# First product of the experts as three products of rounded high and low parts

## What is computed

```python
def _L0_ffn_ref(x, w_g, c_fc, c_proj):          # 8 experts, top 2, 640 places each
    ...
    exp_batches = jnp.einsum('tec,td->ecd', sec_mask, xt)          # rows sorted to the experts
    h = jax.nn.gelu(jnp.einsum('ecd,edf->ecf', exp_batches, c_fc), approximate=False)
    exp_out = jnp.einsum('ecf,efd->ecd', h, c_proj)
    out = cb_weight.reshape(T, N_EXP * cap) @ exp_out.reshape(N_EXP * cap, d)
    ...
```

## Time and profile before

| | us |
|---|---|
| median of 3 runs | 496.49 |
| lowest and highest | 496.16, 497.43 |
| span of the profiled execution | 505.8 |

### The profile page before, as it was taken

How to read it: one execution, slowest core, us unless ns; L and a number is a source line. 1 busy time by engine, 2 the same in 40 slices (tenths; PEclk the granted TensorE clock), 3 DMA queues, 4 the chain that set the end, 5 groups by cost and what they waited for, 6 DMA issues and landing times.

```text
span 505.8 us, 7932 instructions
## 1 busy us (share of the span) xinstructions
PE 434.7 (86%) x2766; PEld 302.8 (60%) x2766; DVE 299.7 (59%) x712; ACT 228.6 (45%) x351; POOL 257.2 (51%) x321
## 2 busy tenths in 40 slices
PE   7887695868778899999989999888966989999980
PEld 6534252425677778888965333335545967888860
DVE  4899899998520313215696999899954201211354
ACT  4867673433110352242167998876842013224220
POOL 5897785898648854565340000022546533455470
PEclk9999996978979999999999999999987899999996
DMA  5455473991342211225613434594011121221266
GB/s 136 141 196 209 143 256 98 330 280 38 75 163 68 74 60 55 78 58 192 189 42 95 99 95 101 143 277 154 28 37 43 38 79 42 63 76 55 73 228 209
DMA packets 50327, 60.87 MB, mean 120 GB/s; under 512 B 7152, under 2 KB 29296, under 8 KB 50288
## 3 DMA queue, kind: packets, MB, share of 16 engines
q1 hardware_dynamic: 42672, 47.50, 31.8%
q0 software_dynamic: 4608, 8.47, 5.2%
q10 hardware_dynamic: 3008, 4.40, 2.7%
HBM read 29.78 MB, written 25.31 MB: 109 GB/s over the span
## 4 chain that ended last, share of the span: by engine, by line
PE 30%; issue 20%; SPq 15%; DMA 6%; DVE 4%; POOL 1%; another core or an unknown queue 1%; ACT 1%; POOLq 0%; ACTq 0%; DVEq 0%
PE ps L1354 26%; SPq L390 12%; SPq L322 3%; PE ps L1510 2%; DMA chosen_y<-ye,y_to 2%; DMA last_got<-chosen_y 1%; DMA got<-chosen_y 1%; PE ps L1358 1%; POOL chosen_y L552 1%; DMA xe<-slots_x 1%; DVE xn L1249 1%; DMA slots_x<-rows_x,put_at 0%; DVE stats L1238 0%; DVE xres L1178 0%
## 5 line engine op out<-in xcount | busy, mean ns | idle before, releaser
L552 POOL DMA_INDIRECT chosen_y<-ye,y_to x80 | 78.8, 985 | 77.0 <-DVE ye L1224 56.1
L729 ACT ACTIVATE hT<-ps 128x640 f32<-128x640 f32 x64 | 45.1, 704 | 86.2 <-issue 53.3
L502 POOL DMA_INDIRECT slots_x<-rows_x,put_at x64 | 62.9, 982 | 41.3 <-issue 19.4
L1358 PE MATMUL ps<-ident 128*128 128x128 f32 x576 | 75.7, 293 | 5.6 <-POOL head_of L423 2.1
L1278 DVE SCALAR_TENSOR_TENSOR feat<-expo,ps 128x1024 f32<-128x1024 f32 x64 | 76.4, 1217 | 3.7 <-ACT expo L858 3.3
L858 ACT ACTIVATE expo<-ps,minus_one 128x1024 f32<-128x1024 f32 x64 | 70.4, 1116 | 12.9 <-PE ps L1354 9.0
L1358 PEld LDWEIGHTS ps<-ident 128*128 128x128 f32 x576 | 70.5, 152 | 8.5 <-issue 3.7
L1354 PE MATMUL ps<-cproj_sb,hT 128*128 128x128 f32 x640 | 74.6, 275 | 0.3
L1354 PEld LDWEIGHTS ps<-cproj_sb,hT 128*128 128x128 f32 x640 | 73.0, 192 | 0.9 <-issue 0.6
L1354 PE MATMUL ps<-xeT,cfc_sb 128*128 128x320 f32 x256 | 71.7, 433 | 2.1 <-DVE xeT L1189 2.1
L1189 DVE COPY xeT<-ps 128x640 f32<-128x640 f32 x16 | 13.2, 825 | 93.6 <-PE ps L1510 46.3
(11 more groups left out here) (230 smaller groups left out, 603.7 us busy)
## 6 DMA issues: line engine op xcount, KB each, us to landing
chosen_y<-empty_rows SPq DMA_DIRECT2D x32, 256.0 KB
decay<-k_rows SPq DMA_DIRECT2D x30, 256.0 KB, 5.4
stk<-part SPq DMA_DIRECT2D x96, 64.0 KB, 2.0
slots_x<-empty_rows SPq DMA_DIRECT2D x16, 325.0 KB, 6.3
xe<-slots_x SPq DMA_DIRECT2D x16, 325.0 KB
cfc_sb<-in_L_ffn_c_fc SPq DMA_DIRECT2D x2, 2048.0 KB
got<-chosen_y SPq DMA_DIRECT2D x8, 256.0 KB
got<-chosen_y ACTq DMA_DIRECT2D x8, 256.0 KB
```

The lines of the kernel that those rows point to most:

```text
L502: pool.indirect_dma_start(out=slots_x[k], out_offset=bass.IndirectOffsetOnAxis(ap=put_at[:, c, kk, t:t + 1], axis=0), in_=rows_x[:, kk * N ...
L552: pool.indirect_dma_start(out=chosen_y[k], out_offset=bass.IndirectOffsetOnAxis(ap=y_to[:, b, i:i + 1], axis=0), in_=ye[:, b, i * D:(i + 1 ...
L729: act.activation(hT[:, b, f, :].rearrange("p (a n) -> p a n", a=2), ps[:, 2 + 2 * (f % 2):4 + 2 * (f % 2), 0:HALF], ACT.Gelu).then_inc(h_r ...
L1358: pe.transpose(ps[:, bank, 0:P], ident[:], ident[:])
```

## The change

The first product takes its operands in the type float32r, which PE multiplies in one record instead of two. To keep the precision, weights and rows are each split into a rounded high part and the rest: high weights by high rows, low weights by high rows, and high weights by low rows are added up in PSUM. ACT rounds (`weights_high`, `rows_high`), DVE subtracts (`weights_low`, `rows_low`), one expert ahead. The split weights of two experts and the low rows lie in the space of `stk`, so its ones are set after the layer's first products. `rows_high` takes the place of the copy to `xeT`; `stack_proj` moves behind expert 2's gelus.

```diff
-            stk = sb("stk", [STK, NB, NG, BK], F32R, mb)
+            room = sb("room", [P, NB * NG * BK], F32R, mb)
+            stk = room[0:STK, :].rearrange("p (c g t) -> p c g t", c=NB, g=NG)
+            cfc_hi = room[:, 0:2 * FF].rearrange("p (b f) -> p b f", b=2)
+            cfc_lo = room[:, 2 * FF:4 * FF].rearrange("p (b f) -> p b f", b=2)
+            xe_lo = room[:, 4 * FF:4 * FF + 2 * CAP].rearrange("p (b n) -> p b n", b=2)
...
-            xeT = sb("xeT", [P, 2, CAP], F32, m)
+            xe_hi = sb("xe_hi", [P, 2, CAP], F32R, m)
...
+        weights_split = lambda s: 2 * s + 1
+        rows_split = lambda s: 2 * s + 2
...
# POOL
-                    pool.memset(stk[3 * GR:STK, :, :, :].bitcast(F32), 1.0).then_inc(stk_ones, 1)
-                    pool.wait_ge(stk_ones, 2)
...
             experts(0)
+            pool.wait_ge(h_mm, NE * NF)
+            pool.memset(stk[3 * GR:STK, :, :, :].bitcast(F32), 1.0).then_inc(stk_ones, 1)
+            pool.wait_ge(stk_ones, 2)
...
# ACT
+                def weights_high(e):
+                    s = k * NE + e
+                    if e == 0:
+                        act.wait_ge(cfc_in, 16 * (k + 1))
+                    if s >= 2:
+                        act.wait_ge(h_mm, (s - 1) * NF)
+                    copy(cfc_hi[:, e % 2, :], cfc_sb[:, e, :]).then_inc(high_ready, 1)
+
+                def rows_high(e):
+                    s = k * NE + e
+                    act.wait_ge(xe_turned, s + 1)
+                    if s >= 2:
+                        act.wait_ge(h_mm, (s - 1) * NF)
+                    copy(xe_hi[:, e % 2, :], flat(ps[:, 0:2, :])[:, 0:CAP]).then_inc(high_ready, 1)
+
+                weights_high(0)
+                rows_high(0)
                 for e in range(NE):
...
                     act.activation(slot_w[:, b, :], xe[:, b, :, D + 1], ACT.Tanh, scale=0.5).then_inc(share_ready, 1)
-                    if s == 2:
-                        stack_proj()
+                    if e + 1 < NE:
+                        weights_high(e + 1)
                     for f in range(NF):
...
                                        ACT.Gelu).then_inc(h_ready, 1)
+                    if e + 1 < NE:
+                        rows_high(e + 1)
+                    if s == 2:
+                        stack_proj()
...
# DVE
-                def turned_in(e):
+                def weights_low(e):
...
+                    dve.wait_ge(high_ready, weights_split(s))
...
-                    dve.tensor_copy(xeT[:, b, :], flat(ps[:, 0:2, :])[:, 0:CAP]).then_inc(xeT_ready, 1)
-
-                turned_in(0)
+                    dve.tensor_tensor(cfc_lo[:, b, :], cfc_sb[:, e, :], cfc_hi[:, b, :].bitcast(F32),
+                                      ALU.subtract).then_inc(low_ready, 1)
+
+                def rows_low(e):
...
+                    dve.wait_ge(high_ready, rows_split(s))
...
+                    dve.tensor_tensor(xe_lo[:, b, :], flat(ps[:, 0:2, :])[:, 0:CAP], xe_hi[:, b, :].bitcast(F32),
+                                      ALU.subtract).then_inc(low_ready, 1)
+
+                weights_low(0)
+                rows_low(0)
                 for e in range(NE):
...
                     if e + 1 < NE:
-                        turned_in(e + 1)
+                        weights_low(e + 1)
...
                     dve.wait_ge(y_to_ready, s + 1)
+                    if e + 1 < NE:
+                        rows_low(e + 1)
...
# PE
-                        pe.wait_ge(xeT_ready, s)
+                        pe.wait_ge(low_ready, rows_split(s - 1))
...
-                pe.wait_ge(cfc_in, 16 * (k + 1))
...
-                    pe.wait_ge(xeT_ready, s + 1)
+                    pe.wait_ge(high_ready, rows_split(s))
                     for f in range(NF):
                         if s * NF + f >= 2:
                             pe.wait_ge(h_ready, s * NF + f - 1)
-                        for a_ in range(2):
-                            ins = mm(ps[:, 2 + 2 * (f % 2) + a_, 0:HALF], cfc_sb[:, e, f * P:(f + 1) * P],
-                                     xeT[:, b, a_ * HALF:(a_ + 1) * HALF])
+                        for n, (w, rows) in enumerate(((cfc_hi, xe_hi), (cfc_lo, xe_hi), (cfc_hi, xe_lo))):
+                            if f == 0 and n == 1:
+                                pe.wait_ge(low_ready, weights_split(s))
+                            if f == 0 and n == 2:
+                                pe.wait_ge(low_ready, rows_split(s))
+                            for a_ in range(2):
+                                ins = mm(ps[:, 2 + 2 * (f % 2) + a_, 0:HALF], w[:, b, f * P:(f + 1) * P],
+                                         rows[:, b, a_ * HALF:(a_ + 1) * HALF], start=n == 0, stop=n == 2)
```

More of the change, by code:

```diff
@@ L207, in program @@
             ("ln_stat", "ln_mv", "ln_std", "ln_rstd", "ln_shift", "ln_out", "xn_turned", "xnT_ready")))
-        wT_mm, wT_ready, wbeta_ready, wv_ready = sem("wT_mm"), sem("wT_ready"), sem("wbeta_ready"), sem("wv_ready")
+        wT_mm, wT_ready, spread_ready = sem("wT_mm"), sem("wT_ready"), sem("spread_ready")
         qk_mm, beta_mm, gate_mm, sq_ready, raw_ready, sumsq_mm = (
@@ L228, in program @@
         ye_out = [sem(f"ye_out{i}") for i in range(2)]
-        xe_turned, xeT_ready, h_mm, h_ready, ye_mm, ye_ready = (
-            sem(n) for n in ("xe_turned", "xeT_ready", "h_mm", "h_ready", "ye_mm", "ye_ready"))
+        xe_turned, high_ready, low_ready, h_mm, h_ready, ye_mm, ye_ready = (
+            sem(n) for n in ("xe_turned", "high_ready", "low_ready", "h_mm", "h_ready", "ye_mm", "ye_ready"))
         rows_made, ids_made, y_to_ready, share_ready = (
@@ L751, in _ @@
             copy(wbeta[:].rearrange("p (h d) -> p h d", d=HD),
-                 wall[:, 3 * D:QKVB].unsqueeze(2).broadcast_to((P, H, HD))).then_inc(wbeta_ready, 1)
+                 wall[:, 3 * D:QKVB].unsqueeze(2).broadcast_to((P, H, HD))).then_inc(spread_ready, 1)
             turned_x(0, 5)
@@ L755, in _ @@
                  wall[:, 2 * D:3 * D].rearrange("p (h i) -> p i h", i=HD).unsqueeze(3).broadcast_to((P, HD, H, HD))
-                 ).then_inc(wv_ready, 1)
+                 ).then_inc(spread_ready, 1)
             square_half(0, 1)
@@ L1181, in experts @@
             def experts(k):
-                def turned_in(e):
+                def weights_low(e):
                     b = e % 2
                     s = k * NE + e
-                    dve.wait_ge(xe_turned, s + 1)
+                    dve.wait_ge(high_ready, weights_split(s))
                     if s >= 2:
                         dve.wait_ge(h_mm, (s - 1) * NF)
-                    dve.tensor_copy(xeT[:, b, :], flat(ps[:, 0:2, :])[:, 0:CAP]).then_inc(xeT_ready, 1)
-                turned_in(0)
+                    dve.tensor_tensor(cfc_lo[:, b, :], cfc_sb[:, e, :], cfc_hi[:, b, :].bitcast(F32),
+                                      ALU.subtract).then_inc(low_ready, 1)
+                def rows_low(e):
+                    b = e % 2
+                    s = k * NE + e
+                    dve.wait_ge(high_ready, rows_split(s))
+                    if s >= 2:
+                        dve.wait_ge(h_mm, (s - 1) * NF)
+                    dve.tensor_tensor(xe_lo[:, b, :], flat(ps[:, 0:2, :])[:, 0:CAP], xe_hi[:, b, :].bitcast(F32),
+                                      ALU.subtract).then_inc(low_ready, 1)
+                weights_low(0)
+                rows_low(0)
                 for e in range(NE):
@@ L1550, in _ @@
             pe.wait_ge(wall_in, 16 * 4)
-            pe.wait_ge(wbeta_ready, 1)
+            pe.wait_ge(spread_ready, 1)
             pe.wait_ge(xnT_ready[0], 1)
@@ L1556, in _ @@
             project_q(0)
-            pe.wait_ge(wv_ready, 1)
+            pe.wait_ge(spread_ready, 2)
             repeat_v(0)
```

## The result

The changed kernel takes 491.77 us (median of 14 runs, 489.33 to 497.2) beside 496.05 us for the kernel before in the same session: a ratio of 0.9935, 95% interval 0.9913 to 0.9957, so 3.2 us less (2.1 to 4.3). The medians themselves lie 4.3 us apart; this text goes by the ratio, which comes with an interval and leaves out the one slow run, at 497.2. The forecast was 491.8. In a second session the same kernel came out at 492.90 beside 494.16, a ratio of 0.9978 (0.9951 to 1.0006), so 1.1 us less (-0.3 to 2.4). So the time is right. The gain is smaller than the 4.7 us forecast, which lies outside both intervals; the two sessions don't agree well on it, and the second alone would not show one. What follows shows why: two of the forecast's steps went another way, in opposite directions.

A forecast was written before the change was run, and what follows sets the result against it. PE was taken to bound the expert layers; 0.58 us gained per later expert, less 1.36 in each first one and a cut at layer 2's end, made 4.7 us: 496.49 to 491.8 us, range 488.3 to 495.2.

The forecast's parts named there:

- The product: First product on PE: each float32r product of 320 columns takes 0.148 us (0.144 to 0.151), six making 0.89 a block.
- rival without extra: First product on PE: 0.133 us a product, by columns alone, so 488.3 us; chance 0.10.
- slower rival: First product on PE: weight loads not overlapped, 0.255 us a product, about 527 us in all; chance 0.06.
- The stop ahead of the third block: First product, each expert: PE stands 0.17 us because the first block's gelu must empty the bank pair.
- Copies, subtractions and memset at nothing: ACT's and DVE's added work mid-layer and POOL's moved memset cost nothing; cover some 2 us, for the memset 1.2.
- The first expert: First expert of each layer: two exposed table loads on ACT make it 1.36 us later (1.30 to 1.39).
- rival of a hidden tail: Table loads on ACT: 1.2 to 1.6 us unrecorded on each of four, 496.5 to 498.3 us; chance 0.03.
- The clock: Rival, first expert: PE's clock falls in its idle time, 1.7 us a layer, 493.5 or 495.2 us; chance 0.23.
- Layer 2's end: Last two experts of layer 2: early adds on DVE hold `ye`, so only 0.5 of 1.16 us gained counts.
- The sum: Both layers: 2.7 us gained in layer 1 and 2.0 in layer 2, together 4.7 us (4.0 to 5.7).
- The loads are not exposed: Rival, first expert: table loads shared or early, it loses only some 0.3 us, so 489.7 us; chance 0.06.

The follow-up runs named there:

- two terms: Changed kernel without the product of high weights by low rows, 16 records in place of 24, all copies and subtractions kept; 483.5 us, ratio 0.978.
- old product: Changed kernel with all copies, subtractions, waits and moved memset, but the first product in float32 as before, one per half; 497.45 us, ratio 1.0058.
- gelu column: Changed kernel plus one gelu of a 128x1 column on ACT ahead of weights_high(0) in both layers; 486.15 us, and 486.33 in another session.
- gap filled: Changed kernel plus 15 dummy transposes on PE between the second and third block of each layer's first expert; 488.64 us, ratio 0.9884.

## Why the prediction came out as it did

**The product: right.** 0.148 us was forecast (0.144 to 0.151), 0.148 measured, so 0.015 of extra on 320 columns beside 0.017 on 512. The rival without extra falls. All weight loads lie under the products, so the slower rival falls too.

**The stop ahead of the third block: right.** 0.17 forecast, 0.17 in the profile, and with two terms 0.47, both from 1.06 between the first block's end and the third's start. Period 8.75 forecast, 8.73 measured.

**Copies, subtractions and memset at nothing: right.** Periods of 9.32 with all of them and the old product. The cover measured 2.84 us where I said some 2. The memset and the normalisation behind it, by POOL's and DVE's timelines, stand against the earlier trace rows:

```profile
238.10 6.93 POOL L587 MEMSET room<- 1x8192 f32 x1
...
246.29 1.34 DVE L1290 TENSOR_SCALAR xn<-xres,mv,rstd 128x128 f32<-128x128 f32 x4
```

It ends at 245.03, 1.26 us ahead of an unchanged normalisation.

**The first expert: right at full clock.** 1.36 us later was forecast; 1.34 and 1.24 were measured (7.50 at full clock in either layer, against 6.16 and 6.26). The chain has ACT's steps in the order and lengths of the forecast. Behind the load the Tanh follows after 0.01 us, so the rival of a hidden tail falls. With it falls the Trainium skill's drain of about 1380 ns (ScalarE: Activation LUTs, "What ACT_TABLE_LOAD costs"), which no load here shows whose next instruction was ready. The same page of the Trainium skill, in its section "Table sets: the hidden batching unit", lists the Tanh with the sets of exp and sigmoid and not with gelu's; here the Tanh ran behind the gelu's load without one of its own, and the gelu column used that.

**The clock: the step that failed.** I gave a fall in the first expert 0.23 and priced one at 1.7 us. The price was right (1.6 measured). The chance was not: with the stop of 1.76 us it fell in three of four first experts, with 2.6 and 3.6 us in four of four. With the stop filled or removed it fell in one of twelve, with the stop of 1.6 (old product) in none of two, in the kernel before in none of four. "Products stand close on both sides" was no argument against it. That the stop raises the chance of a fall is shown, on these few first experts, by taking it away in two ways; that it is the only cause is refuted by the one fall without it, whose cause stays open. With falls in three of four layers the forecast's gain drops by 2.4 us. By these counts the likeliest case was a fall in at least one layer, in the prediction's own prices 493.5 or 495.2.

**Layer 2's end: the step that failed the other way.** Only 0.5 of 1.16 us was to count, because the early adds end at 486.73 and `ye` starts at 487.25. The mechanism exists: in the second profile of the changed kernel `ye` comes 10.85 us after the last transposes, so the last expert gains nothing there. But the row was one draw. Over the profiles of the kernel before, the changed one, the gap filled and the gelu column, the second add of layer 2 starts 8.0 to 10.3 us after the last transposes, late where its rows land late; in layer 1 of the same profiles it starts at 8.0 to 8.1 each time. In the first profile of the changed kernel, with the gap filled and in one of the two of the gelu column all 0.58 us of the last expert counted (10.20 to 10.24 in place of 10.81). The forecast treated a fetch's landing as fixed.

**The sum.** Without falls the layers give 72.89 - 70.09 = 2.80 and 73.00 - 70.12 = 2.88, 5.7 us, where 4.7 was forecast, and the kernel with the gap filled measured 5.7. The difference of 1.0 is layer 2's end (0.66) and first experts and periods a little better than forecast (0.3). Falls take 1.6 each off it: three in four layers leave 3.3, and the ratio says 3.2 in the first session and 1.1 in the second. That the median met the forecast to 0.1 us is luck: one error of 1.0 and one of 2.4 in opposite directions stand behind it. What lies behind each layer varies too: from layer 1's last `ye` to the normalisation were 11.96 and 10.82 us in the two profiles of the kernel before and 11.72 to 12.56 in those of the changed one, the gap filled and the gelu column, so the agreement of 5.7 with 5.7 is good to its interval and no further.

**A rival priced wrongly.** "The loads are not exposed" was put at 489.7, on a first expert that still loses 0.3. With the gelu column it gains 0.5 to 0.6, as the other experts do. PE waits 0.89 us for the copy to `xe_hi` where it waited 1.01 for the one to `xeT`, and the wait for the low rows costs some 0.2. The two loads were worth 1.9 us a layer, and 1.6 more where the clock fell. "Every load in the trace speaks against" was misread: the kernel before has two loads at the Tanh's line for its 16 Tanhs, so all but the first of each layer ran behind gelus without one. That one set serves both could be seen in it.

## What to carry to other kernels

A step put ahead of an activation with its own table moves the load behind the step's wait. Ask in what order the engine meets its first use of each table, and let a column of the last one pull the load forward: here the gain was 8.1 and 8.7 us with it, beside 3.2 and 1.1 without, each kernel in two sessions. A stop such as this one, 1.8 us on PE, should be costed with its fall of the clock as the likely case, and a transfer's landing read from more than one execution before a gain is cut by it. Before work is moved into a stop, look for the wait that it covers where it stands: moving five transposes lost 0.22 us an expert, moving one gained 0.11.

## What the runs showed of the hardware

- A float32r product of 320 columns with a weight load of its own costs 0.148 us at 2.4 GHz; at 1.2 GHz, in the first expert of layer 1, six of them take 1.60 us (165.81 to 167.41), so 0.267 each, which is 320 columns without anything extra.
- A table load costs its 1.28 us and 0.01 to 0.02 to the next instruction; none of the 12 to 14 loads of a profile stands at a copy, and the gelu's table serves the Tanh.
- The clock fell after a stop of 1.76 us three times in four, and cost 1.6 us each time; with stops of 2.6 and 3.6 us it fell four times in four. It fell once in the first expert of a kernel without that stop, behind waits of 1.64 and 1.34 us for scattered rows.
- A fetch of 256 KB landed 8.05 us after the last transposes of layer 2 in one execution and 10.25 in another of the same kernel.
